# Second attention layer of a one-core transformer kernel: how five PSUM banks are divided between two kinds of score

## The chip, the cores and the metric

The kernel runs on one NeuronCore of one Trainium2 chip. The core has a matrix engine (PE; its weight loads are listed apart, as PEld), a vector engine (DVE), a scalar engine (ACT), GpSimd (POOL), and a queue engine (SP) that issues transfers. PE writes its results to eight PSUM banks of 128 partitions x 512 fp32 values, and DVE and ACT read them there. The metric is the device time of one execution in microseconds (us); lower is better.

## The reference, cut to what matters

The program is a chain of four layers on x of shape (8, 512, 256): attention A, a feed-forward layer with experts, attention B, and the feed-forward layer again. The change lies in attention B, an ordinary causal attention with 16 heads of 16 features and rotary positions:

```python
x = x + _L0_attn_b_ref(_layernorm(x), Wq, Wk, Wv, Wo)

def _L0_attn_b_ref(x, Wq, Wk, Wv, Wo):        # B, T, C = 8, 512, 256; H, Dh = 16, 16
    q, k, v = (x @ Wq.T), (x @ Wk.T), (x @ Wv.T)        # each reshaped to (B, T, H, Dh)
    q, k = _apply_rotary(q, cos, sin), _apply_rotary(k, cos, sin)
    scores = jnp.einsum('bhqd,bhkd->bhqk', q, k) * Dh ** (-0.5)
    scores = jnp.where(causal, -jnp.inf, scores)
    attn = jax.nn.softmax(scores, axis=-1)
    out = jnp.einsum('bhqk,bhkd->bhqd', attn, v)
    return out.transpose(0, 2, 1, 3).reshape(B, T, C) @ Wo.T
```

## The kernel before

Attention B is `layer_b`. It works on pairs of heads: 8 batches x 8 pairs = 64 pairs. Every score is computed twice on PE, from q and k that were split into bf16 parts and stacked in SBUF:

- the scores for the maximum, fills named `("s", pair, u)`: queries on the partitions. DVE adds the causal mask and reduces each tile to its (negated) row maximum in `maximum` (L2447: one custom instruction and one read of its accumulator for each tile). Nothing else is done with them;
- the turned scores, fills named `("st", pair, u)`: keys on the partitions. The matmul contracts over three more rows, which hold the negated maximum in three bf16 parts, and a mask matmul (L2676) stands ahead of it in the same bank, so ACT turns the whole bank into probabilities with one exponential (`exponentials`, L2572), from which PE takes the products with v (L2742).

A pair's lower triangle of 128x128 tiles is cut into five units (`UNITS`), of at most 512 columns each, so each unit of each kind is one fill of one bank. A unit of the first kind has one or two matmuls (L2682) of 128 to 512 columns and as many DVE reductions; a unit of the turned kind has the mask matmul and the same one or two matmuls, and one exponential over 512 columns.

Work is laid out in slots, one for each pair. In slot p, PE goes in this order over u = 0 to 4: turned unit u of pair p, then unit u for the maximum of pair p + 7 (`LEAD`). After u = 1 come the early extras (`misc_early`: turning x, projecting q, k and v, the maxima's transposes), after the turned and the plain unit 2 half of the products of a group of four heads (`products`), after u = 3 the late extras (`misc_late`: turning the output of four heads, output projection). All engines run their instructions strictly in this order. ACT's order in a slot is exponential 0, in some slots `return_max`, exponential 1, in some `high`, exponential 2, the copies out of the early extras' banks, exponential 3, in some `middle`, exponential 4, then the copies out of the products' bank and the late extras' banks.

The maximum makes a round trip. A half is four pairs (8 heads). When DVE has its 20 units, POOL splits the maxima (`split_max`, L2541 to L2545), PE turns them in the early extras two slots ahead of the half's first turned slot, ACT copies them (L2615) and issues a DMA to DRAM (L2617). In the slot just ahead of the half, right after exponential 0, ACT waits for that DMA and issues the one that brings the maxima back into the stacked q (`return_max`, L2629). PE waits for its landing at the half's first turned unit. Halves begin at slots 0, 4, 8, and so on, so the waits of ACT stand in slots 3, 7, 11, 15, ... Slots are counted here from 0 (the first with a turned unit) to 63; slots -7 to -1 have scores for the maximum alone, slots 57 to 63 turned scores alone.

Banks: each kind of fill takes its banks in turn. A fill waits until the bank's last reader has finished (`Fills.free`, semaphore `bank_free` of that bank). Banks 0 to 4 hold scores, bank 5 the products, banks 6 and 7 all extras.

Of the kernel before, what the change touches and what calls it, by code (L numbers as in the profile page):

```python
# [101 lines left out]
class Signals:  # L102
# [5 lines left out]
    def sem(self, name):  # L108
        handle = self.stack.enter_context(self.nc.semaphore(name))
        self.numbers.append(handle.num)  # L110
        return handle
# [2112 lines left out]
def layer_b(core, moe, dram):  # L2224
# [4 lines left out]
    with ExitStack() as ctx:  # L2229
# [24 lines left out]
        s = {n: sem("b_" + n) for n in names}  # L2254
# [47 lines left out]
        order, used = [], {"st": 0, "s": 0, "pv": 0, "misc": 0}  # L2302

        def add(kind, name):
            homes = {"st": (0, 1, 2), "s": (3, 4), "pv": (5,), "misc": (6, 7)}[kind]
            order.append((name, homes[used[kind] % len(homes)]))
            used[kind] += 1

        for slot in range(FIRST_SLOT, SLOTS):
            for u in range(len(UNITS)):  # L2310
                if turned_at(slot) is not None:
                    add("st", ("st", slot, u))
                if scored(slot) is not None:
                    add("s", ("s", scored(slot), u))
                if u == 1:
                    for name in misc_early(slot):
                        add("misc", name)
                if u == 2 and 0 in pv_at(slot)[1]:
                    add("pv", ("pv", pv_at(slot)[0]))
                if u == 3:  # L2320
                    for name in misc_late(slot):
                        add("misc", name)
# [549 lines left out]
```

## Time and profile before

| | |
|---|---|
| time, three runs | 2378.61 us median (2374.04 to 2383.83) |
| the profiled execution's own time | 2377.76 us |
| its span on the core | 2375.7 us |
| attention B in it | about 1441 us (first score) to 1937 us |
| PE / DVE / ACT / POOL busy over the span | 92% / 63% / 43% / 28% |

PE busy is not PE at its peak: matmuls are pipelined, and the profile models their ends, about 0.17 us after the engine can take the next. So in dense stretches a short stop of PE does not show as idle PE; the idle time of the weight loads (PEld), which are issued by the same sequencer, shows it, and somewhat more than it. The columns of the views are explained at the rows.

### The profile page before, as it was taken

The page shows a single profiled execution, that of the slowest core. Times are in us where ns is not written, and L with a number is a line of the kernel's source. Part 1 is how long each engine was busy: PE and PEld are TensorE (multiplying, and loading weights), DVE is VectorE, ACT ScalarE, POOL GpSimd, SP SyncE. Part 2 cuts the span into 40 slices and gives each one's busy share as a digit, 9 for nine tenths or more (in the row PEclk, how much of TensorE's full clock was granted, in tenths as well). Part 3 has the DMA queues.
Part 4 walks back from the last instruction along what each step waited for, and adds up shares of the span by engine and source line. Part 5 has one row for each costly group of instructions (what it writes and reads, how often), then busy time and mean ns, then how long its engine had stood idle before and what let it go on. Part 6 is the DMA issues. An engine that isn't in the chain of part 4 may idle for free. (4 is left out here: it accounts for less than half of the span.)

```text
span 2375.7 us, 50326 instructions
## 1 busy us (share of the span) xinstructions
PE 2176.4 (92%) x19611; PEld 1762.4 (74%) x19611; DVE 1491.8 (63%) x3888; ACT 1027.3 (43%) x1986; POOL 676.3 (28%) x768
## 2 busy tenths in 40 slices
PE   7799999999999999898799986899998988988998
PEld 7688888888888888777689973454554557767998
DVE  2565665747565564688656656777777628875665
ACT  4343434333443433444245531555555543433554
POOL 3210110101010100466522223333334115662222
PEclk8899999999999999999999996999999989999999
DMA  7300000000000000421657756555545235114775
GB/s 242 121 19 11 10 10 11 19 2 19 11 10 11 11 2 2 135 64 62 240 168 225 226 148 120 99 89 94 92 83 82 43 98 203 37 45 133 224 224 140
DMA packets 156100, 212.87 MB, mean 90 GB/s; under 512 B 51848, under 2 KB 140192, under 8 KB 150560
## 3 DMA queue, kind: packets, MB, share of 16 engines
q1 hardware_dynamic: 141420, 190.73, 28.3%
q0 software_dynamic: 12864, 17.38, 4.4%
q8 instruction: 158, 2.59, 0.5%
q10 hardware_dynamic: 1584, 1.57, 0.3%
q14 instruction: 74, 0.61, 0.1%
HBM read 141.93 MB, written 67.69 MB: 88 GB/s over the span
## 5 line engine op out<-in xcount | busy, mean ns | idle before, releaser
L2447 DVE CUSTOM_DVE_ANT_0 bank<-bank,b_raw_masks 128x512 f32<-128x512 f32 (+3 forms) x512 | 239.2, 518 | 123.0 <-PE bank L2682 116.0
L2572 ACT ACTIVATE b_probsT<-bank 128x512 f32<-128x512 f32 x320 | 181.0, 603 | 167.6 <-PE bank L2682 136.8
L2161 PE MATMUL bank<-e_hT_hi,k_rwkv 128*128 128x256 f32 x1088 | 221.3, 287 | 2.8 <-DVE e_hT_lo L2065 2.8
L2161 PEld LDWEIGHTS bank<-e_hT_hi,k_rwkv 128*128 128x128 f32 x1088 | 179.7, 193 | 3.3 <-DVE e_hT_lo L2065 3.3
L796 POOL TENSOR_TENSOR probs<-probs,rcp 128x512 f32<-128x512 f32 x64 | 66.9, 1045 | 345.5 <-DVE rcp L665 345.5
L2682 PE MATMUL bank<-b_k_stacked,b_q_stacked 96*128 96x512 bf16 (+3 forms) x512 | 129.5, 317 | 33.8 <-DVE b_neg_max L2447 24.2
L2161 PE MATMUL bank<-e_hT_lo,k_rwkv 128*128 128x256 f32 x544 | 154.5, 284 | 0.0
L2175 PE MATMUL bank<-v_rwkv_hi,e_hidden_hi 128*128 (+1 forms) x544 | 152.8, 281 | 0.4 <-DVE e_hidden_lo L2086 0.4
L2175 PE MATMUL bank<-v_rwkv_lo,e_hidden_hi 128*128 (+1 forms) x544 | 152.3, 280 | 0.0
L2175 PE MATMUL bank<-v_rwkv_hi,e_hidden_lo 128*128 (+1 forms) x544 | 152.2, 280 | 0.0
L2122 ACT ACTIVATE e_relu<-bank,k_bias 128x256 f32<-128x256 f32 x272 | 113.6, 470 | 77.3 <-PE bank L2161 74.3
L2682 PE MATMUL bank<-b_q_stacked,b_k_stacked 99*128 99x512 bf16 (+3 forms) x512 | 122.3, 302 | 0.0
L967 PEld LDWEIGHTS bank<-pi_t,wz 64*64 64x64 f32 x3072 | 97.2, 134 | 32.7 <-issue 23.2
L967 PE MATMUL bank<-pi_t,wz 64*64 64x64 f32 x3072 | 110.4, 221 | 3.5 <-DVE pi_t L707 3.5
L647 DVE TENSOR_TENSOR conv_lo<-bank,conv_hi 128x512 fp32r<-128x512 f32 x64 | 44.3, 692 | 109.6 <-ACT conv_hi L812 109.6
L2084 DVE TENSOR_TENSOR e_square<-e_relu 128x512 f32<-128x512 f32 x136 | 93.9, 691 | 28.2 <-ACT e_relu L2122 22.2
L2161 PEld LDWEIGHTS bank<-e_hT_lo,k_rwkv 128*128 128x128 f32 x544 | 104.9, 193 | 0.0
L2086 DVE TENSOR_TENSOR e_hidden_lo<-e_square,e_hidden_hi 128x512 fp32r<-128x512 f32 x136 | 94.2, 693 | 14.5 <-DVE e_square L2084 0.5
L2175 PEld LDWEIGHTS bank<-v_rwkv_hi,e_hidden_hi 128*128 128x128 f32 x544 | 102.4, 188 | 0.6 <-DVE e_hidden_lo L2086 0.6
L2175 PEld LDWEIGHTS bank<-v_rwkv_lo,e_hidden_hi 128*128 128x128 f32 x544 | 102.6, 189 | 0.0
L2682 PEld LDWEIGHTS bank<-b_k_stacked,b_q_stacked 96*128 96x128 bf16 x512 | 42.9, 99 | 80.4 <-DVE b_neg_max L2447 58.1
L2175 PEld LDWEIGHTS bank<-v_rwkv_hi,e_hidden_lo 128*128 128x128 f32 x544 | 102.3, 188 | 0.0
(362 smaller groups left out, 6128.9 us busy)
## 6 DMA issues: line engine op xcount, KB each, us to landing
k_rwkv<-scratch_k SPq DMA_DIRECT2D x32, 2048.0 KB, 7.3
scratch_b_parts<-b_part SPq DMA_DIRECT2D x93, 128.0 KB, 2.5
b_q_stacked<-scratch_b_parts SPq DMA_DIRECT2D x90, 128.0 KB, 4.3
b_k_stacked<-scratch_b_parts SPq DMA_DIRECT2D x90, 128.0 KB, 4.4
rows<-scratch_rows SPq DMA_DIRECT2D x34, 258.0 KB, 7.9
scratch_rows<-rows SPq DMA_DIRECT2D x16, 516.0 KB, 7.9
x_tokens<-in_x_dram SPq DMA_DIRECT2D x8, 512.0 KB, 7.2
scratch_x_out<-x_tokens SPq DMA_DIRECT2D x8, 512.0 KB, 3.4
```

The costliest lines, as they stand in the source:

```text
L647: nc.vector.tensor_tensor(lo, fills.data(*name)[:], hi.bitcast(F32), ALU.subtract).then_inc(fills.released(*name), 1)
L796: nc.gpsimd.tensor_tensor(probs, probs, spread(rcp1[:, f], NP), ALU.mult).then_inc(s["probs1_done"], 1)
L967: last = nc.tensor.matmul(data[h, j * M:(j + 1) * M], lhs[h, j], rhs[h, j], start=True, stop=True)
L2084: nc.vector.tensor_tensor(flat(sq[:, q % 2]), flat(r[:, q % 2]), flat(r[:, q % 2]), ALU.mult).then_inc(s["square_done"], 1)
L2086: nc.vector.tensor_tensor(flat(h2[1][:, q % SQ_RING]), flat(sq[:, q % 2]), flat(h2[0][:, q % SQ_RING]).bitcast(F32), ALU.subtract).then_in ...
L2122: nc.scalar.activation(r[:, q % 2, n], fl.data("h", q)[:, n * ROWS:(n + 1) * ROWS], ACT.Relu, bias=ff.k_bias[i % 2][:, 2 * c + n:2 * c + n ...
L2161: last = nc.tensor.matmul(data[:, half * ROWS:(half + 1) * ROWS], ff.k_part(i % 2, a)[:, k, at:at + P], hT[b][:, i % 2, k], start=n == 0, ...
L2175: last = nc.tensor.matmul(fl.data("e", i)[:, t * C:(t + 1) * C], h2[a][:, q % SQ_RING, half, t * P:(t + 1) * P], values[b], start=chunk == ...
L2447: last = nc.vector.tensor_tensor_reduce(data[:, at:at + size], data[:, at:at + size], raw_masks[:, T - size:T], -1.0, LARGEST, ALU.add, AL ...
L2572: nc.scalar.activation(probsT[:, ring, u], fl.data("st", pair, u)[:], ACT.Exp, scale=DB ** -0.5).then_inc(fl.released("st", pair, u), 1)
L2682: last = nc.tensor.matmul(data[:, at:at + size], weights[:, tile:tile + P], moving[:, first:first + size], start=not turned and n == 0, st ...
```

## The change

One line. The turned scores take their banks in turn from (0, 1) in place of (0, 1, 2), the scores for the maximum from (2, 3, 4) in place of (3, 4). No instruction is added, removed or moved on any engine; only the bank of each fill, and so the reader that each fill waits for, is another.

```diff
@@ -2302,7 +2302,7 @@
         order, used = [], {"st": 0, "s": 0, "pv": 0, "misc": 0}
 
         def add(kind, name):
-            homes = {"st": (0, 1, 2), "s": (3, 4), "pv": (5,), "misc": (6, 7)}[kind]
+            homes = {"st": (0, 1), "s": (2, 3, 4), "pv": (5,), "misc": (6, 7)}[kind]
             order.append((name, homes[used[kind] % len(homes)]))
             used[kind] += 1
```

On PE, at the start of slot 22, stood before (L2676 opens a turned unit, L2682 with `b_k_stacked` written first is a unit for the maximum; `bank_free2` is the wait for bank 2):

```order
6894 L2676 MATMUL bank<-masks,ident 128x128 [waits bank_free2]
6895 L2682 MATMUL bank<-b_q_stacked,b_k_stacked 128x512
6896 L2682 MATMUL bank<-b_k_stacked,b_q_stacked 128x512 [waits bank_free4]
6897 L2676 MATMUL bank<-masks,ident 128x256 [waits bank_free0]
6898 L2682 MATMUL bank<-b_q_stacked,b_k_stacked 128x384
6899 L2682 MATMUL bank<-b_q_stacked,b_k_stacked 128x128
6900 L2682 MATMUL bank<-b_k_stacked,b_q_stacked 128x384 [waits bank_free3]
6901 L2682 MATMUL bank<-b_k_stacked,b_q_stacked 128x128
```

The same place of PE after the change:

```order
6894 L2676 MATMUL bank<-masks,ident 128x128 [waits bank_free0]
6895 L2682 MATMUL bank<-b_q_stacked,b_k_stacked 128x512
6896 L2682 MATMUL bank<-b_k_stacked,b_q_stacked 128x512 [waits bank_free3]
6897 L2676 MATMUL bank<-masks,ident 128x256 [waits bank_free1]
6898 L2682 MATMUL bank<-b_q_stacked,b_k_stacked 128x384
6899 L2682 MATMUL bank<-b_q_stacked,b_k_stacked 128x128
6900 L2682 MATMUL bank<-b_k_stacked,b_q_stacked 128x384 [waits bank_free4]
6901 L2682 MATMUL bank<-b_k_stacked,b_q_stacked 128x128
```

The instructions stand in the same rows; a turned unit now waits for the exponential of the second turned unit before it (it was the third), and a unit for the maximum for DVE's reductions of the third before it (it was the second).

## Rows read from the trace of the kernel before

**Rows 1.** Busy time by engine in five stretches of attention B (us; x instructions; PEclk granted clock)

```profile
1441.00:1484.00 43.00, 28.55 (x83) 9.48 (x81) 32.70 (x132) 6.10 (x9) 12.02 (x15) 0.61 0.66 116
1484.00:1600.00 116.00, 103.87 (x709) 55.32 (x707) 81.78 (x318) 62.83 (x122) 45.54 (x56) 0.96 0.52 92
1600.00:1833.00 233.00, 212.36 (x1534) 116.69 (x1533) 169.58 (x648) 127.12 (x249) 91.22 (x112) 1.00 0.51 89
1833.00:1888.00 55.00, 48.95 (x376) 27.67 (x374) 37.37 (x147) 29.71 (x58) 11.86 (x18) 1.00 0.37 61
1888.00:1921.00 33.00, 31.34 (x278) 17.43 (x276) 7.69 (x27) 23.10 (x45) 1.13 (x5) 1.00 0.01 3
```

The columns are the stretch, its length, then busy us of PE, PEld, DVE, ACT and POOL, the granted clock as a share of full speed, and the share and GB/s of the DMA engines.

**Rows 2.** Waits in 1600 to 1833 us: total us, times, longest

```profile
ACT b_probsT L2572 <- PE bank L2682: 66.3, 50, 3.2
DVE bank L2447 <- PE bank L2682: 57.5, 56, 1.9
...
ACT b_probsT L2572 <- DMA scratch_b_max<-b_max_rows: 20.1, 8, 3.4
...
PEld bank L2682 <- DVE b_neg_max L2447: 19.3, 39, 0.9
...
PEld bank L2676 <- ACT b_probsT L2572: 5.0, 8, 0.7
...
PEld bank L2682 <- DMA b_k_stacked<-scratch_b_parts: 2.8, 3, 1.2
...
PEld bank L2676 <- DMA b_q_stacked<-scratch_b_max: 1.9, 4, 0.6
```

**Rows 3.** Timeline at the start of slot 22: start, length, engine, work [idle before]

```profile
1644.11 0.60 ACT L2572 ACTIVATE b_probsT<-bank 128x512 f32<-128x512 f32 x1 [0.84 <-PE bank L2682]
...
1644.62 0.22 PE L2676 MATMUL bank<-masks,ident 128*128 128x128 bf16 x1
...
1645.12 0.59 ACT L2572 ACTIVATE b_probsT<-bank 128x512 f32<-128x512 f32 x1
...
1645.60 0.10 PEld L2682 LDWEIGHTS bank<-b_k_stacked,b_q_stacked 96*128 96x128 bf16 x1 [0.88 <-DVE b_neg_max L2447]
...
1645.83 0.27 PE L2676 MATMUL bank<-masks,ident 128*128 128x256 bf16 x1
...
1646.36 0.11 PEld L2682 LDWEIGHTS bank<-b_k_stacked,b_q_stacked 96*128 96x128 bf16 x2 [0.32 <-DVE b_neg_max L2447]
```

**Rows 4.** Timeline, slots 30 to 33: ACT's wait in slot 31, PE around it

```profile
1709.09 0.30 ACTq L2617 DMA_DIRECT2D scratch_b_max<-b_max_rows  x1
...
1713.02 0.28 PE L2676 MATMUL bank<-masks,ident 128*128 128x256 bf16 x1
...
1714.01 1.57 ACT L2572 ACTIVATE b_probsT<-bank 128x512 f32<-128x512 f32 x3 [2.43 <-DMA scratch_b_max<-b_max_rows]
...
1716.32 0.10 PEld L2676 LDWEIGHTS bank<-masks,ident 128*128 128x128 bf16 x1 [0.53 <-DMA b_q_stacked<-scratch_b_max]
...
1724.22 0.39 PE L2682 MATMUL bank<-b_k_stacked,b_q_stacked 96*128 96x512 bf16 x1 [0.84 <-DMA b_k_stacked<-scratch_b_parts]
```

**Rows 5.** Timeline of slot -4: PE's query projection, then DVE's next unit

```profile
1458.25 3.73 PE L2712 MATMUL bank<-b_xnT,wq_b 128*128 128x512 f32 x4
...
1462.44 0.70 DVE L2447 CUSTOM_DVE_ANT_0 bank<-bank,b_raw_masks 128x512 f32<-128x512 f32 x1 [3.07 <-PE bank L2682]
```

**Rows 6.** Waits in 1833 to 1888 us

```profile
PEld bank L2682 <- DVE b_neg_max L2447: 6.9, 12, 1.2
```

**Rows 7.** Waits in 1888 to 1921 us

```profile
ACT b_probsT L2572 <- PE bank L2682: 8.5, 12, 2.3
```

**Rows 8.** Timeline at the start of slot 59, with turned scores alone

```profile
1899.79 0.60 ACT L2572 ACTIVATE b_probsT<-bank 128x512 f32<-128x512 f32 x1 [0.17 <-PE bank L2682]
1899.81 0.27 PE L2676 MATMUL bank<-masks,ident 128*128 128x256 bf16 x1
...
1900.44 0.23 PE L2676 MATMUL bank<-masks,ident 128*128 128x128 bf16 x1
```

## The prediction

> **What bounds the kernel now.** I first cut attention B into stretches and read which engine is full in each. In the steady part PE is busy 212.4 of 233 us, DVE 169.6, ACT 127.1 [rows 1]: PE sets the pace, and only its stops cost time. The steady part holds four batches, 58 us each, so a slot is about 7.3 us. Then I read who stops PE. DVE idles 57.5 us and ACT 66.3 us for want of scores, so neither is full; yet PE's weight loads stop 39 times for a bank that DVE has not read (19.3 us), and 8 times for one that ACT has not read (5.0 us) [rows 2]. The reader should see both numbers as the price of the present split: two banks for the maximum stop PE at the start of nearly every slot, three for the turned scores hardly ever. The stops of weight loads overstate PE's loss; at the one below, 0.88 us of idle loads are about 0.7 us of PE.
>
> Then I took the timeline, because the total does not say what a turned unit would wait for with a bank less.
>
> **The change, part by part.** It removes no work. Four places have an effect.
>
> *Starts of slots.* Between the late extras and the early ones PE runs four units of each kind in a burst, and there the stops lie. Slot 22 [rows 3]: turned unit 0 starts at 1644.62 without a stop. With two banks it waits for the exponential of the unit two before it, 1644.11 + 0.60 = 1644.71, and about 0.05 us of handing over (an exponential ends at 1900.39 and the unit that waited for it starts at 1900.44 [rows 8]): +0.15. The unit for the maximum then starts at 1645.60, after 0.7 us of stop; with three banks its bank has long been free, so it starts at about 1645.05. Turned unit 1 could follow some 0.23 us later, at 1645.28, but waits for the exponential that ends at 1645.12 + 0.59 = 1645.71, so it starts at 1645.77 (0.05 to 0.06 later), against 1645.83 now. The unit for the maximum behind it loses another stop of about 0.2 us (0.32 of idle loads). So 0.9 us of stops go, 0.65 come, and PE is 0.27 us ahead. The stall moves from DVE's bank to ACT's, one instruction on. Where only one stop of 0.3 us goes, 0.2 comes by the same working. Over 39 stops in 32 slots the mean is 0.5 us of idle loads for each [rows 2], so the slot above is among the costlier ones; I take 0.25 us saved in two slots of each batch and nothing in the rest: 0.5 us a batch over 4 of them, less for the others, **-2 us**. Bounds: nothing saved is 0; all of DVE's stops saved and nothing put in their place is 19.3 / 4 = 4.8 us a batch, -38 us over eight; all the new stops and none of the old ones saved is 0.65 us in each of some 56 slots, +36 us. The two ends are one edit seen with one eye; the row at which both are seen gives a value near the middle.
>
> *The slot before each batch.* ACT waits there, behind exponential 0, for the DMA of the maxima: issued at 1709.09, and exponential 1 cannot start until 1714.01, after 2.43 us of idle ACT [rows 4]. With three banks PE has filled units 1, 2 and 3 by then; unit 3 starts at 1713.02. With two banks unit 3 needs exponential 1, which ends at 1714.01 + 0.52 = 1714.53 (three in 1.57 us), so it starts at 1714.6, **1.6 us later**, and the output projection and unit 4 behind it too. ACT's wait is set by the DMA and does not move. Two waits further on take some of this back: PE stops at the next slot for the maxima's return (0.53 us of idle loads, about 0.4 of PE), and in the slot after that for the stacked k (0.84 us) [rows 4]. Both end when a transfer lands that was set off before the delay. Over four batches these two are 1.9 and 2.8 us of idle loads [rows 2], together about 1.1 us a batch. So 0.5 us a batch remain, and with seven such slots (7, 15, ... 55): **+3 us**. Bounds: taken back wholly 0; not at all 7 x 1.6 = +11 us. The other ACT waits of the 20.1 us stand in slots 3, 11, ..., which are longer, and I cost them at nothing; if they block as well, it is another +11.
>
> *Before the first turned slot and after the last batch's projections.* In slots -7 to -1 DVE is the fuller engine (32.7 of 43 us) and PE runs at half clock [rows 1]. A projection holds PE for 3.73 us, DVE has two units in hand and then idles for 3.07 us [rows 5]. With a third bank PE is one unit further when the projection starts, some 0.85 us (0.70 + 0.14 for 512 columns). Two such places, slots -4 and -3: **-2 us**, bounds 0 and -3 (a third place). From 1833 to 1888 us there are few projections, PE stops 12 times for DVE, 6.9 us [rows 6], and DVE is nearly as full; I take a third of it, **-2 us**, bounds 0 and -7.
>
> *Slots 57 to 63.* Turned scores alone: the bank taken away is missed and the bank given is idle. PE is busy 31.3 of 33 us [rows 1]. Slot 59: turned unit 1 starts at 1899.81, but the exponential two before it ends at 1899.79 + 0.60 = 1900.39: +0.63. Unit 2 waits for that same one now, until 1900.44; it would wait for the next, which ends some 0.5 us later: about +0.5 for what follows [rows 8]. ACT waits for PE 12 times there, 8.5 us in all [rows 7], so ACT's work moves back with PE and the same loss comes anew in each slot: 7 x 0.5 = 3.5, and more where ACT has copies ahead of exponential 0 (a copy takes as long as an exponential, some two or three of them): **+5 us**, bounds 0 and +8.
>
> **Sum.** -2 + 3 - 2 - 2 + 5 = +2. Against the profiled execution's 2377.76 us that is 2380; this execution lies 0.85 us under the median of the runs, so **2381 us** is what I expect to be measured.
>
> On the first place: the Trainium skill (Perfetto Trace Analysis, Optimization Strategy) says that the same gap repeating on the engine that should be full can mean too little PSUM for the next tile. Here the trace agrees as far as it names the wait (19.3 us on DVE's bank). By the page alone the gap would go, worth up to the 38 us of the bound; the timeline says that most of it only changes its releaser.
>
> **The rivals.**
> - *Faster, the stops really go.* For it: DVE needs about 0.85 us for each wide unit and an exponential takes 0.60 [rows 3], so the slower reader gets the deeper queue; ACT idles 66.3 us for PE [rows 2]. It decides at turned unit 1 of a slot: if its exponential ends before PE gets there, the 0.65 us are not paid. That happens where ACT has no `middle` or copies ahead of it. If half of the 0.65 is not paid, in some 40 slots, it is -13 us: about **2366 us**. Against: in slot 22 the exponential that counts ends 0.4 us after PE would get there (1645.71 against 1645.28).
> - *Slower, the DMA of the maxima holds PE.* The mechanism of the second place without its taking back, since the landings of which I count were set off late as well: +11, with the tail's 5 and the other gains gone: **2394 us**. It decides at PE's two DMA stops at slots 8, 9, 16, 17, ...: if they keep their length, the delay was not taken back. Against: they end with transfers issued one or more slots before.
> - *Nothing moves.* The gains and losses of each slot cancel and the tail hides: 2378 to 2380. I count it with the forecast.
> - *The clock falls.* Granted clock is 0.61 in the stretch where PE is busy 28.6 of 43 us, 1.00 in the steady one [rows 1]. If stops moved about make it fall (2.4 to 1.2 GHz) for one batch, PE's 53 us of work there would take up to twice as long: **2430 us**. Against: the number and sum of stops stay nearly the same. The Trainium skill (TensorE: Matmul & The Clock Gate, A second HAM failure mode: psum-queue depth-cycling) tells of a kernel whose clock swings because PE pauses at each change of bank; the present kernel has such pauses with 1.00 granted, so the trace does not bear it out.
>
> **How the numbers follow.** Forecast with its own range 2372 to 2389: 0.74 (this takes in "nothing moves"). Faster: 0.11. Slower by the DMA: 0.13. Clock: 0.02. 0.5% is 12 us, about what the measurement can tell from no change. All of the forecast but its edge lies within that; the faster case is mostly beyond 0.5%, the slower one just beyond. The range that leaves 2 in 10 out reaches a little toward both: 2369 to 2392. Faster by over 0.5%: 0.09; within: 0.77; slower: 0.14.
>
> **What would show it.** In the waits of 1600 to 1833 us, DVE's stops of PE near 0 in place of 19.3, ACT's risen from 5 to 15 or 20, their sum about the same; turned unit 3 of slots 15, 23, ... starting right behind exponential 1; PE's DMA stops at the two slots after it gone; the stretch 1888 to 1921 about 5 us longer; granted clock unchanged. The prediction is wrong if a batch is a microsecond or more from 58.4 us either way, which I would first look for in the slots with ACT's wait.

## The result

| | before | after |
|---|---|---|
| median of the runs | 2381.16 us (8 runs, 2374.04 to 2388.00) | 2393.27 us (8 runs, 2388.95 to 2399.55) |
| ratio to before, 95% interval | | 1.0049 (1.0031 to 1.0067) |
| the profiled execution's own time | 2377.76 us | 2399.55 us |
| its span | 2375.7 us | 2397.3 us |

Slower by 12 us, where no measurable change was forecast (2381, range 2369 to 2392). In a second set of 12 runs the changed kernel had 1.0043 (1.0025 to 1.0060). Its profiled execution was the slowest of its eight, so sizes read from it are set beside medians below. Two executions of the whole study, one of before (3490 us, clock 0.56) and one of e7 (2951 us, clock 0.67), ran at a low clock throughout and are in no ratio.

The stretches of after that answer to [rows 1]: the first score comes at 1448.9 us (1441.6 before; nothing ahead of it was changed, and in the profiles of this study it lies anywhere from 1441.4 to 1452.0). Busy time in each stretch, columns as there:

```profile
1449.00:1490.00 41.00, 26.86 (x80) 9.29 (x80) 31.36 (x131) 5.95 (x10) 11.96 (x15) 0.62 0.67 115
1490.00:1606.00 116.00, 101.19 (x705) 53.78 (x703) 81.81 (x316) 61.94 (x121) 45.48 (x56) 0.96 0.52 91
1606.00:1855.00 249.00, 220.32 (x1537) 119.31 (x1536) 170.49 (x649) 127.91 (x249) 91.07 (x112) 0.97 0.50 86
1855.00:1907.00 52.00, 48.34 (x375) 26.91 (x373) 37.42 (x149) 29.89 (x59) 11.83 (x18) 1.00 0.33 54
1907.00:1947.00 40.00, 34.26 (x278) 16.81 (x276) 8.13 (x27) 24.66 (x47) 1.12 (x5) 0.96 0.01 2
```

The same work takes 41 us in place of 43 in front, 249 in place of 233 in the four steady batches, 52 in place of 55 in the last, 40 in place of 33 in the tail. The granted clock, 1.00 in the last three stretches before, is 0.97 and 0.96 in two of them. An estimate from these rows: 249 us at 0.97 and 40 us at 0.96 lack 7.5 and 1.6 us of full clock, so about half of the 16 us by which the steady stretch grew, and a quarter of the 7 us of the tail, is clock in this execution. The waits of the steady stretch, which answer to [rows 2]:

```profile
PEld bank L2676 <- ACT b_probsT L2572: 34.4, 49, 2.4
...
PE bank L2676 <- ACT b_probsT L2572: 13.7, 24, 2.1
ACT b_probsT L2572 <- DMA scratch_b_max<-b_max_rows: 12.1, 5, 3.0
...
PEld bank L2682 <- DMA b_k_stacked<-scratch_b_parts: 6.5, 3, 3.1
```

DVE's stops of PE (19.3 us before) are gone, ACT's have risen from 5.0 to 34.4 us, and those for the stacked k from 2.8 to 6.5 though they are three as before. At an ordinary start of a slot the change does what was worked out from [rows 3]; slot 22 in the timeline of after:

```profile
1654.39 0.23 PE L2676 MATMUL bank<-masks,ident 128*128 128x128 bf16 x1
...
1654.45 0.10 PEld L2682 LDWEIGHTS bank<-b_k_stacked,b_q_stacked 96*128 96x128 bf16 x1
...
1654.75 0.59 ACT L2572 ACTIVATE b_probsT<-bank 128x512 f32<-128x512 f32 x1
...
1655.39 0.10 PEld L2676 LDWEIGHTS bank<-masks,ident 128*128 128x128 bf16 x1 [0.83 <-ACT b_probsT L2572]
1655.39 0.28 PE L2676 MATMUL bank<-masks,ident 128*128 128x256 bf16 x1 [0.34 <-ACT b_probsT L2572]
```

The unit for the maximum follows at once (0.88 us of idle loads before), and turned unit 1 waits until the exponential before it has ended, 1654.75 + 0.59 = 1655.34, and 0.05 more. The stop has moved one instruction on.

Where the time really went is seen from the lengths of the slots: from the exponential of unit 0 of a slot to that of the next, for slots 8n+7, 8n, 8n+1, and the sum of the five behind them.

| batch | before | after |
|---|---|---|
| 7, 8, 9, then 10 to 14 | 5.6, 8.3, 8.4, 38.4 | 4.4, 6.6, **14.7**, 36.8 |
| 15, 16, 17, then 18 to 22 | 5.9, 6.4, 8.7, 37.5 | 6.0, 6.3, **12.7**, 36.8 |
| 23, 24, 25, then 26 to 30 | 6.0, 6.4, 9.0, 37.0 | 6.0, 6.3, **12.8**, 38.4 |
| 31, 32, 33, then 34 to 38 | 6.0, 6.5, 9.1, 37.0 | 7.1, 6.3, 8.3, 37.2 |
| 39, 40, 41, then 42 to 46 | 5.9, 6.5, 8.4, 37.0 | **9.6**, 6.3, 8.3, 36.8 |
| 47, 48, 49 | 6.0, 6.6, 9.4 | **9.8**, 6.3, 8.3 |

A five of 38.4 has one slot (11, 19, 27, ...) that is 10.2 us long in place of 8.6 or 8.7. That is the clock too, and it is no work of the split. In these slots PE stops for 1.14 to 1.19 us, a few times for 1.48, for the normalized x (`b_xn`) in either split; in some of them, at places that differ from profile to profile, the granted clock falls to its lower level behind the stop. The windows of before around slot 11, then one of after in slot 27:

```profile
1562.60:1566.10 3.50, 2.08 (x16) 1.20 (x13) 3.21 (x11) 1.21 (x3) 0.89 (x1) 1.00 1.12 195
1566.10:1569.50 3.40, 3.40 (x25) 1.53 (x24) 1.61 (x8) 1.89 (x5) 0.00 (x0) 0.50 0.49 107
...
1697.50:1701.00 3.50, 3.50 (x26) 1.57 (x25) 2.09 (x8) 2.17 (x4) 0.00 (x0) 0.52 0.43 130
```

Without such a fall, five ordinary slots gain 0.2 us. The loss stands in two places besides the tail, and it is not the same one in the early and the late batches.

*Late batches.* Timeline of slot 39 in after, the place of [rows 4]:

```profile
1788.05 1.09 ACT L2572 ACTIVATE b_probsT<-bank 128x512 f32<-128x512 f32 x2 [2.75 <-DMA scratch_b_max<-b_max_rows]
...
1788.71 0.28 PE L2676 MATMUL bank<-masks,ident 128*128 128x256 bf16 x1 [1.83 <-ACT b_probsT L2572]
...
1789.27 3.35 PE L2717 MATMUL bank<-wo_b,b_attT 128*128 128x256 f32 x8
```

Turned unit 3 starts behind exponential 1, after PE has stood for 1.83 us. That was foreseen. What follows was not: the output projection takes 3.35 us. The windows around it, with the granted clock behind POOL's column:

```profile
1784.00:1789.00 5.00, 2.83 (x30) 1.24 (x29) 2.82 (x11) 2.25 (x5) 1.16 (x1) 1.00 1.11 173
1789.20:1792.70 3.50, 3.50 (x13) 2.59 (x11) 0.88 (x4) 0.60 (x1) 0.00 (x0) 0.56 0.56 104
1793.00:1797.00 4.00, 3.96 (x23) 1.77 (x24) 2.84 (x12) 2.23 (x5) 0.00 (x0) 0.99 0.89 101
```

After the stop the clock falls from 2.4 to about 1.2 GHz (1.00 to 0.56 over the window) for some 3.5 us; the eight matmuls pay 1.4 us for it (1.94 us at full clock, in the experiment without the stop below).

*Early batches.* Timeline of slot 17 in after:

```profile
1615.38 0.10 PEld L2682 LDWEIGHTS bank<-b_k_stacked,b_q_stacked 96*128 96x128 bf16 x1 [3.08 <-DMA b_k_stacked<-scratch_b_parts]
1615.39 0.47 PE L2682 MATMUL bank<-b_k_stacked,b_q_stacked 96*128 96x512 bf16 x1 [2.74 <-DMA b_k_stacked<-scratch_b_parts]
```

PE stands 2.74 us for the stacked k (4.34 and 2.74 us in slots 9 and 25), and here too the clock falls with the stop:

```profile
1606.00:1618.00 12.00, 9.22 (x54) 5.01 (x54) 9.99 (x40) 4.91 (x10) 5.08 (x10) 0.90 0.55 91
```

The transfers that stack the halves were issued late, because a store ahead of them landed late. SP's queue in the timeline, at the start of slot 14, and behind it the packets by queue in the view of the DMAs for the stretch between the two issues, 1594.31 to 1599.01 (packets, MB, share of the engines):

```profile
1594.31 1.31 SPq L2348 DMA_DIRECT2D scratch_b_parts<-b_part  x3
1599.01 1.27 SPq L2331 DMA_DIRECT2D b_q_stacked<-scratch_b_parts  x3
```

```profile
q1 hardware_dynamic: 432, 0.39, 25.3%
q8 instruction: 1, 0.02, 1.9%
```

SP can stack once the three stores have landed: 4.70 us after the first was issued, against 2.76 in before (1587.91 and 1590.67 there). One packet of queue q8, 16 KB of instructions, begins while the third store is under way; by the records of the packets it begins 0.7 us ahead of the time at which that store lands elsewhere. The same stands in slots 6, 14 and 22 of after. In before the packet begins 0.2 to 0.3 us ahead of the landing (slots 6 and 14) or 5 us ahead of it (slot 22), and nothing is late. (The expectations below name these three stores by slots 4, 12 and 20, from whose start they count the 17 to 19 us to them.)

### The profile page after: what moved, and what is told of

Same layout as the page of the kernel before. It is cut to its first block and busy times, and to the rows that moved or that the text cites. A ratio compares the mean times of both kernels' runs of the same rounds, so it can differ in the third digit from the quotient of the medians.

```text
span 2397.3 us, 50326 instructions
## 1 busy us (share of the span) xinstructions
PE 2188.4 (91%) x19611; PEld 1766.8 (74%) x19611; DVE 1488.7 (62%) x3888; ACT 1027.9 (43%) x1986; POOL 675.9 (28%) x768
## 5 line engine op out<-in xcount | busy, mean ns | idle before, releaser
L2572 ACT ACTIVATE b_probsT<-bank 128x512 f32<-128x512 f32 x320 | 183.0, 602 | 187.2 <-PE bank L2682 162.5
L2682 PE MATMUL bank<-b_k_stacked,b_q_stacked 96*128 96x512 bf16 (+3 forms) x512 | 128.6, 317 | 21.4 <-DMA b_k_stacked<-scratch_b_parts 11.8
L2682 PE MATMUL bank<-b_q_stacked,b_k_stacked 99*128 99x512 bf16 (+3 forms) x512 | 124.4, 304 | 0.0
L2676 PE MATMUL bank<-masks,ident 128*128 128x256 bf16 (+1 forms) x320 | 83.4, 261 | 33.7 <-ACT b_probsT L2572 25.7
L2676 PEld LDWEIGHTS bank<-masks,ident 128*128 128x128 bf16 x320 | 31.1, 97 | 109.7 <-ACT b_probsT L2572 64.9
L2086 DVE TENSOR_TENSOR e_hidden_lo<-e_square,e_hidden_hi 128x512 fp32r<-128x512 f32 x136 | 94.2, 692 | 14.5 <-issue 0.5
## 6 DMA issues: line engine op xcount, KB each, us to landing
k_rwkv<-scratch_k SPq DMA_DIRECT2D x32, 2048.0 KB, 12.7
```

What stands on the lines that cost most here:

```text
L2086: nc.vector.tensor_tensor(flat(h2[1][:, q % SQ_RING]), flat(sq[:, q % 2]), flat(h2[0][:, q % SQ_RING]).bitcast(F32), ALU.subtract).then_in ...
L2572: nc.scalar.activation(probsT[:, ring, u], fl.data("st", pair, u)[:], ACT.Exp, scale=DB ** -0.5).then_inc(fl.released("st", pair, u), 1)
L2676: nc.tensor.matmul(region, ident16[:], src, start=True, stop=False, skip_group_check=True)
L2682: last = nc.tensor.matmul(data[:, at:at + size], weights[:, tile:tile + P], moving[:, first:first + size], start=not turned and n == 0, st ...
```

## The experiments

All ratios are to the kernel before, run on the same chip among the others. A difference of two ratios is less certain than either of them: about 0.2% either way, 5 us.

| kernel | median us | runs | ratio | 95% |
|---|---|---|---|---|
| e1: before, maxima's return on SP | 2381.70 | 12 | 1.0002 | 0.9991 to 1.0014 |
| e2: after, the same | 2386.43 | 12 | 1.0010 | 0.9997 to 1.0023 |
| e3: after, three turned banks in the tail | 2386.93 | 12 | 1.0017 | 1.0004 to 1.0030 |
| e5: after, output projection earlier | 2392.37 | 6 | 1.0043 | 1.0028 to 1.0058 |
| e7: after, 128 waits | 2388.74 | 7 | 1.0034 | 1.0019 to 1.0048 |
| e8: before, 16 waits | 2382.04 | 12 | 1.0001 | 0.9986 to 1.0016 |
| e9: e2 and e3 together | 2381.12 | 12 | 0.9996 | 0.9983 to 1.0010 |
| e10: e9 with 128 waits | 2375.09 | 12 | 0.9978 | 0.9962 to 0.9993 |
| e11: e1 with 128 waits | 2385.66 | 12 | 1.0005 | 0.9991 to 1.0020 |
| e12: e10 with five banks at both ends | 2374.92 | 12 | 0.9964 | 0.9952 to 0.9975 |
| e13: e7, slots 8n+7 with the split of before | 2384.77 | 11 | 1.0008 | 0.9998 to 1.0017 |
| e14: before, 32 waits | 2384.83 | 8 | 1.0007 | 0.9992 to 1.0022 |
| e15: after again | 2395.21 | 12 | 1.0043 | 1.0025 to 1.0060 |
| e16: e7 again | 2391.68 | 8 | 1.0043 | 1.0019 to 1.0066 |

**ACT's wait for the maxima: e1 and e2.** In both splits the DMA that brings the maxima back, and the wait for their store, move from ACT's queue to SP's.

```diff
+                    if side == 1:
+                        return_max(half - 2)
                     sp.wait_ge(s["parts_stored"], (at - 1) * 48)
...
                             exponentials(slot, u)
-                        if u == 0:
-                            for n, f in steps_at(slot - 1, FRONT["max"]):
-                                return_max(n, f)
```

> The old banks (three turned, two for the maximum), but the maxima's return transfer and the wait for their store stand in SP's order, not in ACT's, so no exponential stands behind that wait. Theory A (the loss of the change comes mostly from ACT's wait for the maxima's transfer, behind which two banks of turned scores run out): the old kernel has only small stops there (turned units 1 and 2 and one plain unit of the slot ahead of a batch, about 0.45 us each, partly taken back by the later transfer waits), so 0 to -7 us, ratio 0.997 to 1.000. Rival B (the loss comes from stacked k landing later in some batches, which has nothing to do with ACT): no change, 1.000, unless SP's queue itself is delayed, then above 1.

> The changed banks with the same move of the return transfer to SP. Theory A: the slot ahead of each batch is again as long as before (about 6.0 us between the exponentials 0, not 9.6 to 9.8 as in two batches), the granted clock does not fall there, and what is left of the loss is the tail with turned scores alone, 5 to 6 us: ratio to the old kernel 1.002 to 1.003. Rival B: batches still take 61 us and more because plain unit 0 of the slot after a batch's first waits 2 to 3 us for stacked k: ratio 1.004 to 1.005.

With three turned banks ACT's wait costs nothing (1.0002), with two it costs 9 us (1.0049 to 1.0010): that is the interaction that the second place of the prediction spoke of. The ratio of e2 is better than either theory had it, and the edit is broader than that place, since it takes ACT's waits of slots 3, 11, ... away as well. In e2 slots 39 and 47 are 6.2 and 6.1 us long, but 7, 15 and 23 are 7.6 to 8.0: PE stops 2.1 to 3.7 us there for the maxima's return, which in SP's queue now stands behind the held stores (in e10, without held stores there, slots 15 and 23 are 6.0).

**The tail: e3.** Only slots 57 to 63 get the third bank back.

```diff
-            homes = {"st": (0, 1), "s": (2, 3, 4), "pv": (5,), "misc": (6, 7)}[kind]
+            homes = {"st": (0, 1) if kind != "st" or name[1] + LEAD < PAIRS_ALL else (0, 1, 2), "s": (2, 3, 4), "pv": (5,), "misc": (6, 7)}[kind]
```

> The changed banks up to slot 56, and turned scores on banks 0, 1 and 2 in slots 57 to 63, where no scores for the maximum are left. If the tail costs what its span says (34.0 us before, 40.4 after), this gives back 5 to 6 of the 12 us: ratio to the old kernel 1.0025. Rival: what the tail loses is gained behind it (the last output projection waits for other work anyway): ratio stays 1.005.

The tail, from the first exponential of slot 56 to the end of the last, is 34.2 us in it, 34.0 in before, 40.3 in after; the runs give 7.6 us (0.32%). In after, slot 60 is 7.8 us long (4.5 before), and the windows show the clock go down once more, at a place where PE had waited 1.46 us for an exponential:

```profile
1907.00:1920.00 13.00, 11.88 (x103) 5.32 (x101) 5.39 (x21) 8.76 (x17) 1.12 (x5) 1.00 0.01 3
1920.00:1933.00 13.00, 10.75 (x78) 5.74 (x78) 1.05 (x3) 6.67 (x13) 0.00 (x0) 0.87 0.02 4
```

Of the seven profiles with this tail three have that fall (after, e2, e13: 40.3 to 40.4 us) and four have not (e5, e7, e15, e16: 38.8 to 39.0 us). So the tail costs 4.8 us, and 1.6 more where the clock falls.

**The projection ahead of the stop: e5.** In slots 8n+7 the output projection is issued before turned unit 3, not behind it, so that PE has work there.

```diff
-                        if u == 3:
+                        if u == (2 if filler(slot) else 3):
```

> The changed banks; in the slot ahead of each batch PE does the output projection (8 matmuls, 1.9 us) ahead of turned unit 3 in place of behind it, so PE has work while ACT waits for the maxima's transfer. Theory A: the stop of PE at turned unit 3 (1.8 us where ACT's wait is longest) shrinks to nothing, the projection no longer runs at half clock (1.9 us in place of 3.35), so batches in which this happened are 3 us shorter: ratio to the old kernel about 1.003 to 1.004, as the tail's 6 us stay. Rival B: ratio 1.005, batches 61 us and more all the same.

Slots 39 and 47 are back at 6.4 and 6.0 us, yet the total is only 0.06% better, within the intervals. The net is smaller than these two slots show, since with the delay gone the taking back goes too: slots 33, 41 and 49 are 9.0, 9.0 and 9.7 us long in place of 8.3, and slots 31 to 55 together 177.9 in place of 181.0 us. Such a 3 us the six runs cannot tell from nothing. The early batches were nearly as long as in after (slots 9, 17, 25: 15.7, 10.3, 14.1 us). So the slot before each batch isn't the whole of it: a second cause acts in the early batches.

**The packets of instructions: e7, e8, e14.** Waits of TensorE on a semaphore long reached stand ahead of attention B's first transposes. They do no work; two of them make one instruction (the trace of e7 has 64 more than that of after), so 128 move all that follows in TensorE's program by 64 instructions.

```diff
-                pe.wait_ge(core.ident_loaded, 16)
+                for _ in range(129):
+                    pe.wait_ge(core.ident_loaded, 16)
                 keep_awake(core, spare, 6)
```

> The changed kernel with 128 more waits of TensorE on a semaphore long reached, ahead of attention B's first transposes; they add 64 instructions of 64 bytes to TensorE's stream and no work. In the trace of the changed kernel the third part of the rotated scores' operands (SP's store in slots 4, 12, 20) lands 3.4 to 3.8 us after its issue instead of 1.8, and each time a 16 KB packet of queue q8 (instruction) begins while it is under way (19.0 to 19.1 us after the slot's start). Theory 1, the packet holds the store: with 64 instructions more each q8 packet comes a quarter of its distance earlier (about 4.7 us), the three stores land in 1.8 us again, PE's stops for the stacked k in slots 9, 17, 25 fall from 4.5, 2.9, 2.9 us to below 1, and these three slots get 3 to 4 us shorter each. Total 2384 to 2389, ratio 1.001 to 1.003 against before. Theory 2, the new split delays the store itself: nothing changes, the three stores land late again, total 2391 to 2394. The waits themselves cost under 1 us, since TensorE waits for the statistics there.

Theory 1 held for its mechanism; the ratio is above the 1.001 to 1.003 that it gave. SP's queue in e7, at the same place of the program, and the packets between its two issues (1587.49 to 1590.23):

```profile
1587.49 1.31 SPq L2348 DMA_DIRECT2D scratch_b_parts<-b_part  x3
1590.23 2.71 SPq L2331 DMA_DIRECT2D b_q_stacked<-scratch_b_parts  x6
```

```profile
q1 hardware_dynamic: 432, 0.39, 42.6%
```

2.74 us in place of 4.70, no packet of q8, and slots 9, 17 and 25 are 9.2, 8.3 and 8.6 us long. But now slots 15, 23, 31 are 7.1 to 7.3 us and slots 39 and 47 are 9.8 and 10.0: the early batches, no longer held by the stacked k, meet ACT's wait for the maxima. That waits of TensorE move these packets shows whose instructions they are. The Trainium skill (Advanced Engine Details and Errata, ISA Cache) gives an engine's instruction cache lines of 16 KB, 256 instructions; the packets of q8 in the trace are of that size, 0.02 MB each.

> The kernel before with 16 such waits (8 instructions more). In its trace the q8 packet of slot 12's store begins 19.43 us after the slot's start, just before the third part has landed (19.75), and that of slot 4's at 17.11 (landed 17.31); 8 instructions earlier is about 0.5 us. Theory 1 (the packet holds the store): the third parts of slots 4 and 12 land about 2 us later than before, slots 9 and 17 are 2 to 4 us longer, with three banks for the turned scores as they were; total 2384 to 2388, ratio 1.001 to 1.003. Theory 2 (the split does it): all stores land in 1.8 us, total 2381 to 2382, ratio 1.000.

Inconclusive: the packets stayed nearly where they were (17.10 and 19.38 us after the starts of slots 4 and 12, for 17.11 and 19.43). So the test was made again with 32 waits.

> The kernel before with 32 waits (16 instructions more); with 16 waits the q8 packets had not moved (17.10 and 19.38 us after the starts of slots 4 and 12). Theory 1 (a packet of q8 that begins before the third part has landed holds it): they now begin 0.5 to 1.2 us earlier, at about 16.3 and 18.5, and the third parts of slots 4 and 12 land at 18.5 and 21.5 in place of 17.3 and 19.7, with slots 9 and 17 longer by 2 to 4 us. Theory 2: they land at 17.3 and 19.7 whatever the packet does. Total 2382 to 2388.

Half of it came. At slot 4 the packet now begins at 16.58 and the third store lands at 18.70 in place of 17.31, with the split of before. SP's queue and the packets from 1533.9 to 1536.5:

```profile
1532.15 1.30 SPq L2348 DMA_DIRECT2D scratch_b_parts<-b_part  x3
1536.31 2.69 SPq L2331 DMA_DIRECT2D b_q_stacked<-scratch_b_parts  x6
```

```profile
q1 hardware_dynamic: 159, 0.14, 16.4%
q8 instruction: 1, 0.02, 2.5%
```

4.16 us; the same two issues of before are 2.77 apart (1527.24 and 1530.01). At slot 12 the packet stayed at 19.45 and the store landed in time. The delay shows in slots 7 and 8 (7.0 and 9.1 us for 5.6 and 8.3, PE stops 2.87 us for the maxima's return) and not, as expected, in slot 9 (8.4 us), and the total is not measurably longer. So a store is held with the split of before too when a packet begins there, and the split only decided where the packets fall.

**Two and three causes undone: e9, e10, e11.** The edits are those of e2 and e3, then with the 128 waits; e11 is e1 with the waits, as their control.

> The changed kernel with two of its places undone: the maxima's return and its wait on SP in place of ACT, and three banks for the turned scores in slots 57 to 63. Alone they gave ratios of 1.0010 and 1.0017 where the change has 1.0049. If the ACT block and the tail are the loss (theory 1), what is left is the late stores of the early batches less the gains at the starts of slots: total 2379 to 2383, ratio 0.999 to 1.0005. If the two overlap (theory 2: both only shift PE against the same landing), the sum gives no more than either alone: 2385 to 2387, ratio 1.0015 or more.

> The kernel with the maxima's return on SP and three banks in the tail, with the 128 waits as well. If the q8 packets are what makes the early batches long (theory 1), the three waits for the maxima's return and the stacked k at slots 8 to 25 go, 2 to 3 us each: total 2373 to 2379, ratio 0.997 to 0.999; then two banks for the turned scores in the steady slots are worth some microseconds by themselves. Rival: the steady slots gain nothing, and with all three losses undone the ratio is 1.000.

> The kernel before with the maxima's return on SP and the 128 waits: what the best kernel so far (ratio 0.9978) has beside the new split. Theory 1, the gain is the split's: here nothing is gained, since in before no packet of q8 held a store and the return on SP alone gave 1.0002: 2380 to 2384, ratio 0.9995 to 1.001. Theory 2, the gain is of the waits or of SP: 2374 to 2378, ratio 0.997 to 0.999, and the split itself is worth nothing.

Undone together, the losses go one after the other (1.0049, two undone 0.9996, three undone 0.9978), and the control gains nothing (1.0005). Two undone give 0.53%, where each alone gave 0.39 and 0.32; whether they overlap or scatter did that the runs cannot tell. The control also has a held store, with the split of before: in slot 26, where a packet begins 0.8 us ahead of the usual landing, the third store takes 3.65 us for 1.83, and no slot behind it is longer. What is left, 5 us against before and 6 against the control, is the gain of the third bank for the maximum. Of that the batch with few projections (slots 48 to 55) shows most: 50.9 us, against 54.4 in before and 53.5 in e11 (50.6 to 54.1 in all profiles with the new split there, 53.5 to 57.3 in those with the old).

**The slot before each batch alone: e13.** With the 128 waits, the split of before in slots 7, 15, ... 55 only; each fill takes the bank of its kind that was used longest ago, which elsewhere is the same rotation.

```diff
+            if slot % PAIRS_B == PAIRS_B - 1 and 0 <= slot < PAIRS_ALL - 1:
+                homes = {"st": (0, 1, 2), "s": (3, 4)}.get(kind, homes)
+            bank = min(homes, key=lambda home: lately.get(home, -1))
```

> The changed kernel with the 128 waits, and in slots 7, 15, ... 55 alone the split of before (three banks for turned scores, two for the maximum); ACT still waits for the maxima's DMA there and the tail has two banks. Theory 1, turned unit 3 behind ACT's wait is the mechanism: these slots are 5.9 to 6.2 us long as before, in place of 7.1 to 7.3 and 9.8 to 10.0, and the clock stays at 1.00 there; the total falls from 2388.8 by 5 to 9 us to 2380 to 2384, ratio 0.999 to 1.001. Theory 2, it is ACT's wait itself that the slots pay: no change, 2388 to 2390.

Theory 1 held, but for one slot. Timeline of slot 39, where ACT waits 3.00 us for the same DMA (L2679, L2720 and L2575 are L2676, L2717 and L2572 of the kernel before):

```profile
1777.41 0.28 PE L2679 MATMUL bank<-masks,ident 128*128 128x256 bf16 x1
...
1777.97 1.94 PE L2720 MATMUL bank<-wo_b,b_attT 128*128 128x256 f32 x8
...
1778.90 2.07 ACT L2575 ACTIVATE b_probsT<-bank 128x512 f32<-128x512 f32 x4 [3.00 <-DMA scratch_b_max<-b_max_rows]
```

Turned unit 3 starts at 1777.41, before the DMA has landed, the projection takes 1.94 us, and slots 7, 15, 23, 31, 39 are 6.0 to 6.1 us; slot 47 is 7.2 us (the clock at 1.00; PE stops 0.87 us for an exponential and 0.42 us for the maxima's return). Against e7 it is worth 6 us (1.0034 to 1.0008), against its repetition e16 8 us. The granted clock there:

```profile
1775.00:1782.00 7.00, 6.30 (x52) 4.12 (x52) 4.83 (x19) 4.00 (x9) 1.16 (x1) 1.00 0.85 141
```

The clock's part is not one of the profiled execution alone. The granted clock of the whole execution, in the mean of all runs in the ratios, is 0.965 in e13, 0.963 in e7 and 0.962 in e16: an estimated 5 and 8 us of lost time, about what e13 is worth against each of the two.

**A version that beats both: e12.** e10, and where one kind of scores stands alone it takes all five banks.

```diff
+            homes = {"st": (0, 1) if slot + LEAD < PAIRS_ALL else (0, 1, 2, 3, 4), "s": (2, 3, 4) if slot >= 0 else (0, 1, 2, 3, 4), "pv": (5,), "misc": (6, 7)}[kind]
```

> The kernel of ratio 0.9978 with all five banks for the scores for the maximum in slots -8 to -1 and all five for the turned scores in slots 57 to 63, where the other kind has no scores. In front DVE is the fuller engine and waited 3.07 us beside one projection; two banks more cover such a wait for 1.7 us: 2 to 3 us less over slots -4 and -3. At the end PE is busy 31.3 of 33 us, so at most 1 to 2 us. Theory 1: 2371 to 2374, ratio 0.996 to 0.997. Rival: in front the next slots wait for the stacked halves (a DMA) whatever DVE does, and nothing is gained: 0.998.

0.9964, 8.6 us faster than before. In its profile the front (first score to first exponential) is 39.4 us for 42.1 in e10, the tail 33.2 for 34.2. The tail repeats within 0.1 us; fronts scatter by 4 us between profiles. The intervals of e10 and e12 overlap, so the last step is likely, not shown.

**The size of the packets' price: e15 and e16.** The changed kernel and e7 once more.

> The changed kernel unchanged, for a second profiled execution and a narrower interval, beside its twin with 128 waits on the same chip. The price of the packets of q8 is open: from first score to last output the two profiled executions differ by 11.4 us (510.5 and 499.1), the medians by 4 (ratios 1.0049 and 1.0034), and the changed kernel's profiled execution was the slowest of its eight. Theory 1, the price is that of the slots (three of them 3 to 5 us longer, 2 to 3 us given back in slots 15, 23, 31): ratio 1.006 to 1.007, 7 us or more above the twin. Theory 2, it is smaller, since other scatter lies on top in the one profile: the slots 9, 17, 25 are 12 to 15 us long again, but first score to last output is 500 to 505 and the ratio 1.004 to 1.005.

> The changed kernel with the 128 waits, as before (1.0034). Theory 1: 1.003 to 1.004, first score to last output 499 to 501, 7 us or more under its twin without them. Theory 2: the same, but 3 to 5 us under the twin.

The profiled executions repeat: from first score to last output 510.5 and 510.7 us without the waits, 499.1 and 498.7 with them (before 495.2); slots 9, 17, 25 are 14.5, 14.4, 11.9 us in e15 and 8.3, 8.3, 8.6 in e16. The medians don't: 4.5 us in the first pair, 3.5 in the second, and the second pair's ratios are equal. So in the executions that were profiled the packets cost 12 us, in the others on the mean 0 to 5. Part of the 12 is the clock: from slot 0 to the last exponential its lower level was granted for 30 and 27 us without the waits, for 15 and 13 us with them, an estimated 7 us of lost time. The other executions do not have that difference: the mean clock of the whole execution was 0.961 and 0.962 without the waits, 0.963 and 0.962 with them, where the profiled ones had 0.958 twice and 0.963 to 0.964. Why the profiled ones differ, whether the packets fall elsewhere in the rest or cost less there, no trace shows; it stays open. e16 shows too that the fall of the clock is not in every such slot: slot 39 was 7.2 us long there, slots 15 and 47 were 9.6 and 9.9. In e3 slots 39 and 47 had stops of 1.72 and 2.16 us without a fall and were 7.8 and 8.2 us long, so the stop alone makes them some 2 us longer and the clock the rest.

## Why the prediction was wrong

It held that nothing measurable would change, and named a range that ends 1 us under what was measured. Term by term:

- *Starts of slots, -2.* Right. 0.2 us in the five ordinary slots of a batch, the stop moved one instruction on. The rival that the stops really go (2366) is out.
- *Slot before each batch, +3.* This is the term that failed. The wait was right: unit 3 waits for exponential 1, with a stop of 1.8 us where 1.6 was worked out. The taking back came too: the stops for the stacked k at slots 33, 41, 49 are gone, 8.3 us in place of 8.4 to 9.4. What was missing is that the clock goes down behind the stop while the output projection runs, a cost that the term has at nothing. Slots 39 and 47 grew by 3.7 and 3.8 us, not 1.6; where the clock stayed up, in e3, by 1.9 and 2.2. Nor was the delay the same in each of the seven slots: in after slot 31 grew by 1.1 us, slots 15 and 23 by nothing, and slots 7 and 55 became 1.2 us shorter; in e7, without the held stores, slots 15 and 23 grew as well (7.1 and 7.2 us). By runs the term is 6 us (e13 against e7) to 9 (e2 against after), where +3 was forecast.
- *Front, -2.* Not resolved: 40.8 us for 42.6, but over all profiles the front is 38.0 to 42.1 us with the new split and 40.4 to 42.6 with the old.
- *Slots 48 to 55, -2.* Right in sign, a little low: 51.2 us for 54.4.
- *Tail, +5.* Right: 4.8 us, and 6.4 where the clock falls, as it did in this profile; 7.6 by runs (e3).
- *Not in the sum at all:* the packets of instructions, +12 in the profiled executions, 0 to 5 by medians.

With the measured sizes, -2 + 6 (to 9) - 2 - 3 + 7 and 0 to 5 is +6 to +14; measured were +12 and, by e15's ratio, +10. Each of these sizes is uncertain by some 5 us where it comes from runs, so that the sum fits proves little; what each term is rests on its own experiment.

The rival "slower by the DMA of the maxima" gave 2394, which is about the time, but for a reason that the trace denies: it took the delays as not taken back, and in the late batches they were. (In slots 9, 17 and 25 PE's stops did grow, but by the held stores.) The rival "the clock falls" had 2 in 100, since the number and sum of stops would stay the same, and it was priced as one whole batch at the lower clock. The sum of the waits for a bank rose from 24 to 34 us of idle loads, but the clock followed single stops and not the sum: in the steady stretch of after four of its five falls stand at stops of 1.8 us and more, which before had none of there, and the fifth at a stop for `b_xn` that before has too. Before had already shown such a fall, in slot 11 (the rows above), just ahead of the steady stretch whose 1.00 the prediction went by. So this rival named the right thing at a wrong size: some 3.5 us at a time, five times in the steady stretch, not one whole batch. The signs that were named in advance pointed right: the granted clock was to stay and did not, and a batch was not to be a microsecond from 58.4 us and was 61 to 65.

## What to carry to other kernels

A buffer more or less has to be priced where its reader is held up by something slow (here a DMA wait in the queue of the engine that empties the bank) and where its kind of work stands alone, not at the average place. In the slots before a batch the third bank of the turned scores was worth 6 to 9 us and in the tail 5 to 8; at ordinary starts of slots the bank was worth a little more on the other side. A long new stop on TensorE is priced at its length plus what the matmuls behind it lose when the clock falls, here 1.4 to 1.6 us. A loss in the profiled execution is compared with the medians and with the granted clock of the other runs before it is believed at its full size. When a loss sits in only some of the batches, compare the landing of each store with the packets of instructions: shifting the program by a few dozen instructions that do nothing tells within one run whether that is the cause.

## What the runs showed of the hardware

- In slots 6, 14 and 22 a 16 KB packet of instructions on queue q8 that began 0.4 to 1.2 us before a 128 KB store would land went with a landing 1.4 to 2.2 us late (after, e2, e3, e5, e9, e14, e15). Beginning 0.2 to 0.4 us before, it did nothing in before, e1, e8 and e14, and cost 1.9 us once in e9 (slot 22). What tells these apart is open.
- The granted clock in slots 8 to 62 of the sixteen profiles: of PE's 28 stops of 1.75 us and more (by the trace), 24 had a fall to the lower level in them or within 2 us behind them; of the 101 stops of 1.0 to 1.3 us, 19 had. After the stops of 1.83 and 2.74 us it was 0.56 in the 3.5 us behind the first and 0.90 in the 12 us around the second.
- What one fall costs is seen where the stop is the same with it and without it: slots 11, 19, 27, ..., mostly 8.6 to 8.7 us long with a stop of 1.14 to 1.17 us, were 9.9 to 10.3 us long with such a stop and a fall.
